# RWKV attention and GELU feed-forward on one core: the preparation in another order with common scales, the mix for V first in three steps, and three last steps with orders of their own

## The chip, the core and the metric

The program runs on one core of a Trainium2 chip. The metric is the device time of one launch in microseconds (us). A core has five engines that run side by side: TensorE (PE, matmuls and transposes; its weight loads are listed as PEld), VectorE (DVE), ScalarE (ACT), GpSimd (POOL) and SyncE (SP, which here only issues DMAs). They meet through semaphores: an instruction may wait for a count and may raise one when it is done.

## What is computed

x is 4 sequences of 2048 tokens with 512 channels, in float32. Two layers are added to it. The first is an RWKV attention with 32 heads of 16 channels, in chunks of Q = 64 tokens; the second is a feed-forward layer with 2048 hidden units.

```python
x = x + attention(layernorm(x))
x = x + ffn(layernorm(x))

def attention(x):                        # xx is the token before, minus x
    xk, xv, xr, xg = (x + xx * time_maa[m] for m in "kvrg")
    r, k, v = xr @ Wr.T, xk @ Wk.T, xv @ Wv.T      # split in 32 heads
    g = silu(xg @ Wg.T)
    w = exp(-exp(time_decay)); ws = w ** Q; wk = w ** (Q - 1 - i); wb = w ** i
    # per chunk of 64 tokens, carried on by the state:
    att = rc @ kc * w_mat                # w_mat: powers of w below the diagonal, time_faaaa on it
    yc = att @ vc + rc @ state * wb
    state = ws * state + kc * wk @ vc
    return (groupnorm(y) * gamma + beta) * g @ Wo.T

def ffn(x):
    D = gelu(float16(x) @ W0.T + bias0)
    return float16(float16(D) @ W1.T + bias1)
```

## The kernel before

**Tiling.** The 8192 tokens go in nb = 32 blocks of BT = 256 (NT = 2 tiles of 128). Products in float32 precision are made of three float16 passes over a high and a low part (`PASSES`); ACT writes the high part (`..._hi`), DVE or POOL the low one (`..._lo`).

**Preparation (`prepare`).** A block of its own runs ahead of the steps. It loads the five attention weights (`raw`; K_, R_, V_, G_, O_ in this order), transposes them on PE into three PSUM buffers `tp` of 128x1024 each (half a weight), and ACT and DVE write them scaled to `WT`. A scale is a power of two from the largest sum of squares: ACT squares and sums a weight (`act_square`), POOL takes the maximum over partitions (`pool_most`), DVE makes the scale in six small steps (`dve_scale`). ACT also makes the decay tables with Exp (`act_exps`: 16 pieces of 128x64 and three small ones), which DVE finishes in `dve_tables`. The first block's layer norm, transposes (`pe_X`, `act_xT`) and mixes for K and R are made here too. The steps begin when all engines are done with this block.

**Steps.** `steps` runs over n = 0 to nb + 2. Step n does the attention of block n, the tail (group norm, gate, Wo, residual) of block n - 1, the first 12 of 16 weight units of the feed-forward of block n - 2 (`pe_up` 0 to 7, `pe_down` 0 to 3), and its last four units (`pe_down` 4 to 7) in step n + 1. So steps 32, 33 and 34 have no attention: step 32 has a tail and feed-forward work, step 33 feed-forward work, step 34 only the last four downs. In steps 0 and 1 the feed-forward weights are transposed and scaled in sixteen pieces (`pe_prepare`, `act_prepare`, `dve_prepare`), stored to DRAM and read back from step 2 on.

**Order.** It is written out by hand for each engine: `pe_step`, `dve_step`, `act_step`, `pool_step`, `sp_step`. In `dve_step` the first loop interleaves the small steps of the next block's layer norm (`dve_ln`), the mixes for V and G (`dve_mix(n, 2, ...)`, `dve_mix(n, 3, ...)`), `dve_K_lo` and the group norm of the block before (`dve_normalize`); `mix_lo(n, 2)`, for which `pe_V` waits, comes behind the loop. The mix buffers alternate, so the mix for V takes the one that K had.

**DMA.** The SP queue issues in order and waits in order. Feed-forward weights come in units of 512 KB through a ring of 5 (`sp_weights`, each waits until the unit five before it is used up); `sp_fx` transposes the normalised input `xh` to `xT`, for which `pe_up` 0 waits; the output of block n - 3 is stored from `x1`, and x is loaded into the same buffer for the next tail.

**PSUM.** `F` has two banks, used by up j in turn (j % 2), by the downs for the two token tiles t, and emptied by `act_gelu` and `dve_e`.

## Time and profile before

| what | value |
| --- | --- |
| median of 3 runs | 2199.86 us (2199.13 to 2201.25) |
| the profiled execution, device time | 2201.86 us |
| its span, first to last instruction | 2200.0 us |
| PE busy | 2099.5 us (95%) |
| DVE busy | 1878.6 us (85%) |
| ACT busy | 1077.8 us (49%) |
| POOL busy | 382.4 us (17%) |
| chain that ended last | PE 89%, DVE 2%, issue 1% |
| DMA | 437.53 MB, mean 199 GB/s |

The profiled execution took 2.0 us more than the median, and 1.9 us of its time lie outside the span. In a row of the timeline stand the start, the duration, the engine, the line of the kernel, the operation with its tiles, and in brackets how long the engine was idle before and what it waited for. Rows of the same kind that follow each other are merged (x4).

### The profile page before, as it was taken

To read this page: it belongs to the slowest core of one execution; us is meant where nothing else is said; L and a number is where in the kernel's file an instruction comes from. 1 tells how busy PE (TensorE), PEld (TensorE's weight loads), DVE (VectorE), ACT (ScalarE), POOL (GpSimd) and SP (SyncE) were. 2 spreads that over 40 slices of the span, in tenths; PEclk is the share of its full clock that TensorE was granted. 3 is DMA by queue.
4 is the path that set the end of the run, shared out by engine and by line. 5 is a ranking of instruction groups with operands and counts; after the bars stand their busy time and mean duration, and the time that the engine had idled before them with its cause. 6 is when DMAs were issued, how large, how long until landed. Compare 5 with 4: busy or idle time off the path is not lost.

```text
span 2200.0 us, 59109 instructions
## 1 busy us (share of the span) xinstructions
PE 2099.5 (95%) x24288; PEld 1508.5 (69%) x24288; DVE 1878.6 (85%) x4352; ACT 1077.8 (49%) x1882; POOL 382.4 (17%) x336
## 2 busy tenths in 40 slices
PE   3767999999999999999999999999999999999998
PEld 3555777776677777667777766777776677777664
DVE  6788988888998888899888889988888998888861
ACT  6554455545445554444555444455544445554441
POOL 1111112111111211111121111112111211211110
PEclk8888999999999999999999999999999999999999
DMA  6544566676556666655666665566666556666666
GB/s 202 163 154 147 177 202 213 215 216 205 179 184 200 215 214 216 205 181 183 201 214 214 217 201 185 181 201 215 214 217 201 182 182 203 214 214 208 198 215 206
DMA packets 282651, 437.53 MB, mean 199 GB/s; under 512 B 123536, under 2 KB 160912, under 8 KB 282384
## 3 DMA queue, kind: packets, MB, share of 16 engines
q1 hardware_dynamic: 280752, 433.55, 62.6%
q8 instruction: 193, 3.16, 0.6%
q14 instruction: 74, 0.61, 0.1%
q10 hardware_dynamic: 1632, 0.21, 0.1%
HBM read 316.24 MB, written 25.17 MB: 155 GB/s over the span
## 4 chain that ended last, share of the span: by engine, by line
PE 89%; DVE 2%; issue 1%; DMA 0%; ACT 0%; POOL 0%; POOLq 0%; ACTq 0%; SPq 0%; DVEq 0%
PE F L825 21%; PE F L839 20%; PE B L656 11%; PE B L805 7%; PE YT L684 7%; PE sc L656 7%; PE YT L656 3%; PE sc L714 3%; PE YT L735 2%; PE YT L778 2%; PE YT L754 2%; PE sc L697 1%; PE YT L738 1%; PE B L258 1%; PE YT L258 1%
## 5 line engine op out<-in xcount | busy, mean ns | idle before, releaser
L825 PE MATMUL F<-xT,ring 128*128 128x256 f16 x4096 | 489.1, 273 | 5.3 <-DMA xT<-xh 5.3
L839 PE MATMUL F<-ring,hT 128*128 128x512 f16 x2048 | 481.6, 379 | 4.8 <-ACT hT L1279 1.2
L825 PEld LDWEIGHTS F<-xT,ring 128*128 128x128 f16 x4096 | 396.7, 98 | 67.0 <-issue 6.8
L839 PEld LDWEIGHTS F<-ring,hT 128*128 128x128 f16 x2048 | 193.2, 98 | 209.0 <-issue 9.3
L247 ACT ACTIVATE mix<-mixf 128x1024 f16<-128x1024 f32 x128 | 135.2, 1056 | 326.7 <-DVE mixf L219 212.9
L1279 ACT ACTIVATE hT<-F,b,f_rho 128x256 f16<-128x256 f32 x512 | 260.6, 563 | 41.8 <-PE F L825 41.8
L219 DVE SCALAR_TENSOR_TENSOR mixf<-dx,maa,xnT 128x256 f32<-128x256 f32 x512 | 271.2, 556 | 0.1
L656 PE MATMUL B<-mix,WT 128*128 128x256 f16 x2304 | 270.2, 274 | 0.0
L1395 POOL TENSOR_TENSOR Shl<-S,Shl 128x512 f16<-128x512 f32 x128 | 153.8, 1202 | 655.0 <-ACT Shl L1246 655.0
L656 PEld LDWEIGHTS B<-mix,WT 128*128 128x128 f16 x2304 | 224.2, 98 | 36.5 <-issue 0.2
L251 DVE TENSOR_TENSOR mix<-mixf,mix 128x1024 f16<-128x1024 f32 x128 | 196.3, 1534 | 0.0
L1246 ACT ACTIVATE Shl<-S 128x512 f16<-128x512 f32 x128 | 80.1, 626 | 236.1 <-DVE S L1041 131.8
L656 PE MATMUL sc<-mix,WT 128*128 128x256 f16 x1536 | 181.6, 276 | 10.8 <-PEq L434 10.8
L684 PE MATMUL YT<-WT,mix 128*128 128x512 f16 x768 | 180.4, 386 | 10.2 <-DVE mix L251 10.2
L1018 DVE TENSOR_TENSOR att<-att 128x512 f16<-128x512 f32 x256 | 178.4, 736 | 7.5 <-ACT att L1240 7.4
L1012 DVE TENSOR_TENSOR att<-sc,wmask 128x512 f32<-128x512 f32 x256 | 164.2, 683 | 20.7 <-PE sc L714 20.7
L656 PEld LDWEIGHTS sc<-mix,WT 128*128 128x128 f16 x1536 | 151.9, 99 | 43.1 <-issue 11.3
L1400 POOL TENSOR_TENSOR x<-e,x 128x512 f32<-128x512 f16 x64 | 73.0, 1161 | 603.8 <-DVE e L1092 603.8
L805 PE MATMUL B<-WT,yg 128*128 128x512 f16 x768 | 176.2, 379 | 0.1
L1240 ACT ACTIVATE att<-att 128x512 f16<-128x512 f32 x256 | 148.5, 630 | 36.7 <-DVE att L1012 35.7
L684 PEld LDWEIGHTS YT<-WT,mix 128*128 128x128 f16 x768 | 76.0, 99 | 96.6 <-DVE mix L251 10.7
L805 PEld LDWEIGHTS B<-WT,yg 128*128 128x128 f16 x768 | 75.0, 98 | 83.9 <-DVE x L984 0.3
(168 smaller groups left out, 2955.4 us busy)
## 6 DMA issues: line engine op xcount, KB each, us to landing
ring<-w_dram SPq DMA_DIRECT2D x512, 512.0 KB, 4.3
kx<-kT SPq DMA_DIRECT2D x96, 256.0 KB, 2.4
rx<-rT SPq DMA_DIRECT2D x96, 256.0 KB, 4.2
xa<-in_L_attn_x SPq DMA_DIRECT2D x32, 512.0 KB, 7.4
vbd<-vN SPq DMA_DIRECT2D x256, 64.0 KB, 3.7
x<-in_L_attn_x SPq DMA_DIRECT2D x32, 512.0 KB, 5.2
out<-x SPq DMA_DIRECT2D x32, 512.0 KB, 4.8
ring<-in_L_ffn_W SPq DMA_DIRECT2D x10, 512.0 KB, 8.8
```

Of the source, the lines that this page charges most:

```text
L219: last = eng.scalar_tensor_tensor(out=mixf[:, m % 2, g, :], in0=dx[:, g, :], scalar=maa[:, m, g:g + 1], in1=xnT[:, g, 1:BT + 1], op0=ALU.m ...
L251: eng.tensor_tensor(mix[:, m % 2, 1, :, :], mixf[:, m % 2, :, :], mix[:, m % 2, 0, :, :], ALU.subtract).then_inc(s_ml, 1)
L656: mm = eng.matmul(out[:, gg * BT:(gg + 1) * BT], WT[:, w, a, kk, rows(g)], mix[:, m % 2, b, kk, :], start=(i == 0 and kk == 0), stop=(i == ...
L684: mm = eng.matmul(Y[:, t, :], mix[:, 0, a, kk, rows(t)], WT[:, V_, b, kk, :], start=(i == 0 and kk == 0), stop=(i == 2 and kk == G - 1))
L805: mm = eng.matmul(B[:, :], yg[:, a, kk, rows(t)], WT[:, O_, b, kk, :], start=(i == 0 and kk == 0), stop=(i == 2 and kk == G - 1))
L825: mm = eng.matmul(F[:, j % 2, i * BT:(i + 1) * BT], ring[:, use % RING, i, a * C + kk * P:a * C + (kk + 1) * P], xT[:, :, kk, :], start=(k ...
L839: mm = eng.matmul(F[:, t, :], hT[:, k, rows(t)], ring[:, use % RING, i, a * C:(a + 1) * C], start=(k == 0 and a == 0), stop=(k == NH - 1 a ...
L1012: eng.tensor_tensor(att32[:, x, :], sc[:, x, :], wmask[:, 8 * x:8 * x + 8, :].rearrange("p q i -> p (q i)"), ALU.mult).then_inc(s_am, 1)
L1018: eng.tensor_tensor(att[:, c % 2, 1, C * x:C * x + C], att32[:, x, :], att[:, c % 2, 0, C * x:C * x + C], ALU.subtract).then_inc(s_al, 1)
L1240: eng.activation(att[:, c % 2, 0, C * x:C * x + C], att32[:, x, :], ACT.Copy).then_inc(s_ah, 1)
L1279: eng.activation(hT[:, k, :], F[:, j % 2, i * BT:(i + 1) * BT], ACT.Gelu, bias=b0[:, k:k + 1], scale=f_rho[:, j:j + 1]).then_inc(s_h, 1)
L1395: eng.tensor_tensor(Shl[:, b, 1, :], S[:, :], Shl[:, b, 0, :], ALU.subtract).then_inc(s_Sl, 1)
```

## The change

In the preparation the scales are made for two groups, K with R and V with G and O (`TOGETHER`), so POOL has 2 reductions in place of 5 and DVE 2 chains of six small steps in place of 5. A weight's ACT pass to `WT` waits for its group's chain. ACT's Exp pieces move from the end to the front, in two halves; the transposes of x stand behind those of K on PE; DVE makes the decay tables ahead of the second scale chain, and the factors from the scales (`dve_factors`) behind it.

ACT, preparation, before (`junk,sums<-raw` is a square, `WT<-tp` and `WT<-YT` a half weight, `xa` the normalised block, `wmask` the Exp pieces):

```order
L227 ACTIVATE xa<-xa,ln_n,ln_r 128x512 x2
L238 ACTIVATE xnT<-B 128x4x128
L238 ACTIVATE xnT<-YT 128x4x128
L350 ACTIVATE junk,sums<-raw 128x2048 x2
L247 ACTIVATE mix<-mixf 128x1024
L369 ACTIVATE WT<-tp,scl 128x1024 x2
L247 ACTIVATE mix<-mixf 128x1024
L350 ACTIVATE junk,sums<-raw 128x2048
L369 ACTIVATE WT<-YT,scl 128x1024
L369 ACTIVATE WT<-tp,scl 128x1024
```

and now:

```order
L389 ACTIVATE wmask<-tabs,ep 128x64 x8
L352 ACTIVATE junk,sums<-raw 128x2048
L228 ACTIVATE xa<-xa,ln_n,ln_r 128x512 x2
L352 ACTIVATE junk,sums<-raw 128x2048
L239 ACTIVATE xnT<-B 128x4x128
L239 ACTIVATE xnT<-YT 128x4x128
L389 ACTIVATE wmask<-tabs,ep 128x64 x8
L393 ACTIVATE wb<-wb 128x32
L394 ACTIVATE wk<-wk 128x32
L395 ACTIVATE ws<-ec 128x4
L375 ACTIVATE WT<-tp,scl 128x1024 x2
```

The square of K stands ahead of the norm, that of R ahead of the copies of x's transposes, and the Exp pieces that came ahead of the last weight stand in two halves at the front.

DVE, the end of the preparation and the start of step 0, before (`L431` is the last factor, `L219` a mix for V):

```order
L431 TENSOR_SCALAR out_scale<-out_scale 128x1
L434 UNCONDITIONAL_BRANCH
L1556 UNCONDITIONAL_BRANCH
L189 BN_STATS bn<-xa 128x6
L219 SCALAR_TENSOR_TENSOR mixf<-dx,maa,xnT 128x256
L189 BN_STATS bn<-xa 128x6
L219 SCALAR_TENSOR_TENSOR mixf<-dx,maa,xnT 128x256
L193 BN_AGGR mv<-bn 128x2
```

and now (`L383` is the low part of half a weight, `L435` to `L447` the factors, `L220` a mix, `L252` a low part of a mix, `L1003` K's low part):

```order
L447 TENSOR_SCALAR out_scale<-out_scale 128x1
L383 SCALAR_TENSOR_TENSOR WT<-tp,scl,WT 128x1024
L383 SCALAR_TENSOR_TENSOR WT<-YT,scl,WT 128x1024
L383 SCALAR_TENSOR_TENSOR WT<-tp,scl,WT 128x1024 x2
L383 SCALAR_TENSOR_TENSOR WT<-YT,scl,WT 128x1024
L383 SCALAR_TENSOR_TENSOR WT<-tp,scl,WT 128x1024
L450 UNCONDITIONAL_BRANCH
L1647 UNCONDITIONAL_BRANCH
L220 SCALAR_TENSOR_TENSOR mixf<-dx,maa,xnT 128x256 x4
L190 BN_STATS bn<-xa 128x6 x2
L194 BN_AGGR mv<-bn 128x2 x2
L1003 SCALAR_TENSOR_TENSOR kT<-sc,kT 128x512
```

The factors stand ahead of the last six low parts of weights instead of behind them, and the four mixes for V stand together at the front of the step. Behind K's low part follow one small step and the low part of the mix for V, which stood behind the whole loop before. The same holds in steps 1 and 2.

PE, from the end of step 31 to the end, before (`L839` are downs, 8 matmuls each; `L825` ups, 16 each; `L697` the transposes of y; `L805` a half of Wo):

```order
L839 MATMUL F<-ring,hT 128x512 x40
L825 MATMUL F<-xT,ring 128x256 x32
L697 MATMUL sc<-ident,y 128x128 x8
L825 MATMUL F<-xT,ring 128x256 x96
L805 MATMUL B<-WT,yg 128x512 x12
L839 MATMUL F<-ring,hT 128x512 x16
L805 MATMUL B<-WT,yg 128x512 x12
L839 MATMUL F<-ring,hT 128x512 x48
L825 MATMUL F<-xT,ring 128x256 x128
L839 MATMUL F<-ring,hT 128x512 x64
```

and now:

```order
L880 MATMUL F<-ring,hT 128x512 x40
L723 MATMUL sc<-ident,y 128x128 x8
L851 MATMUL F<-xT,ring 128x256 x96
L831 MATMUL B<-WT,yg 128x512 x12
L851 MATMUL F<-xT,ring 128x256 x16
L831 MATMUL B<-WT,yg 128x512 x12
L851 MATMUL F<-xT,ring 128x256 x16
L880 MATMUL F<-ring,hT 128x512 x64
L851 MATMUL F<-xT,ring 128x256 x128
L880 MATMUL F<-ring,hT 128x512 x32
L867 MATMUL F<-ring,hT 128x512 x32
```

The transposes of y stand ahead of all ups, both halves of Wo ahead of the downs, and the last 32 matmuls go tile by tile. On the SP queue the transpose of `xh` stands in steps 32 and 33 ahead of the weight units instead of behind three of them, and the last store is two of 256 KB. On DVE, step 32 has the group norm ahead of `dve_e`; the last residual sum is made by DVE (a tile at a time) instead of POOL. In every step the first down waits for the last two GELU pieces only at its second tile.

The diff, cut:

```diff
+TOGETHER = ((K_, R_), (V_, G_, O_))
...
-        def pool_most(eng, u):
-            eng.wait_ge(s_sum, ORDER.index(u) + 1)
...
+        def pool_most(eng, k):
+            at = columns(TOGETHER[k])
+            eng.wait_ge(s_sum, ORDER.index(TOGETHER[k][-1]) + 1)
+            eng.partition_all_reduce(sums[:, at], sums[:, at], P, bass.bass_isa.ReduceOp.max).then_inc(s_all, 1)
...
+        def dve_ep(eng):
+            eng.wait_ge(s_e0, 1)
...
             @block.tensor
-                for t in range(NT):
-                    pe_X(eng, 0, t)
...
+                    if u == K_:
+                        for t in range(NT):
+                            pe_X(eng, 0, t)
...
             @block.vector
                 for k in range(LN_STEPS):
                     dve_ln(eng, 0, k)
+                    if k == NT - 1:
+                        dve_ep(eng)
                 eng.memset(xnT[:, :, 0:1], 0.0).then_inc(s_carry, 1)
                 dve_exponents(eng)
+                dve_scale(eng, 0)
                 eng.wait_ge(s_maa, 64)
                 dve_dx(eng, 0)
-                for m in range(2):
-                    for g in range(G):
-                        dve_mix(eng, 0, m, g)
-                for u in ORDER:
-                    dve_scale(eng, u)
+                for g in range(G):
+                    dve_mix(eng, 0, 0, g)
+                dve_lo(eng, K_)
+                for g in range(G):
+                    dve_mix(eng, 0, 1, g)
+                mix_lo(eng, 0, 0)
+                dve_lo(eng, R_)
+                dve_tables(eng)
+                dve_scale(eng, 1)
+                mix_lo(eng, 0, 1)
+                dve_factors(eng)
+                for u in (V_, G_, O_):
                     dve_lo(eng, u)
...
     def pe_down(eng, f, j):
-        if j == 0:
-            eng.wait_ge(s_h, NH * (f + 1))
...
+                if k == 0:
+                    eng.wait_ge(s_h, NH * (f + 1) - 2 * (NT - 1 - t))
...
+    def pe_after_attention(eng, n):
+        for j in range(4, 8):
+            pe_down(eng, n - 3, j)
+        pe_yT(eng, n)
+        for j in range(6):
+            pe_up(eng, n, j)
+        pe_Wo(eng, n, 0)
+        pe_up(eng, n, 6)
+        pe_Wo(eng, n, 1)
+        pe_up(eng, n, 7)
+        for j in range(4):
+            pe_down(eng, n - 2, j)
...
     def dve_step(eng, n):
-        if not att_n:
+        if n > nb:
             dve_e(eng, n - 3)
+        early = n <= 2
         for k in range(LN_STEPS):
+            if early and k == 0:
+                for g in range(G):
+                    dve_mix(eng, n, 2, g)
             if ahead:
                 dve_ln(eng, n + 1, k)
-            if att_n:
+            if early:
+                if k in (3, 9):
+                    dve_K_lo(eng, n, (3, 9).index(k))
+                elif k == 4:
+                    mix_lo(eng, n, 2)
+                elif 5 <= k < 9:
+                    dve_mix(eng, n, 3, k - 5)
+            elif att_n:
...
     def sp_step(eng, n):
+        if n >= nb and ff:
+            sp_fx(eng, n - 2)
         if late:
             sp_weights(eng, use)
             sp_weights(eng, use + 1)
             sp_weights(eng, use + 2)
-        if ff:
+        if n < nb and ff:
             sp_fx(eng, n - 2)
```

## Rows read from the trace of the kernel before

**Rows 1.** Windows of us: busy us and (xcount) of each engine, PEclk, DMA share, GB/s:
```profile
222.00:252.00 30.00, 29.84 (x455) 21.18 (x455) 28.97 (x50) 15.67 (x28) 5.89 (x5) 1.00 0.56 191
```

**Rows 2.** Timeline of ACT in the preparation: start us, us, engine, line, operation:
```profile
11.26 1.52 ACT L227 ACTIVATE xa<-xa,ln_n,ln_r 128x512 f32<-128x512 f32 x2 [3.13 <-DVE ln_n L204]
...
13.41 0.60 ACT L238 ACTIVATE xnT<-B 128x512 f32<-128x512 f32 x1 [0.63 <-PE B L258]
...
16.78 1.91 ACT L350 ACTIVATE junk<-raw 128x2048 f32<-128x2048 f32 x1
...
18.69 1.04 ACT L247 ACTIVATE mix<-mixf 128x1024 f16<-128x1024 f32 x1
...
20.45 2.12 ACT L369 ACTIVATE WT<-tp,scl 128x1024 f16<-128x1024 f32 x2 [0.72 <-DVE scl L301]
...
38.94 3.92 ACT L383 ACTIVATE wmask<-tabs,ep 128x64 f32<-128x64 f32 x16
```

**Rows 3.** R's four loads (ns, first and last issue), and the last one's landing:
```profile
L342 SPq DMA_DIRECT2D raw<-in_L_attn_Wr x4: 603/604/1688, 9.0 to 12.1; - x4
...
raw<-in_L_attn_Wr SPq DMA_DIRECT2D x1, 256.0 KB, 3.9
```

**Rows 4.** Timeline of DVE at the end of the preparation:
```profile
45.50 1.28 DVE L377 SCALAR_TENSOR_TENSOR WT<-tp,scl,WT 128x1024 f16<-128x1024 f32 x1
...
49.57 0.15 DVE L419 TENSOR_TENSOR gn_eps<-rho 128x1 f32<-128x1 f32 x1
...
50.65 0.15 DVE L431 TENSOR_SCALAR out_scale<-out_scale 128x1 f32<-128x1 f32 x1
```

**Rows 5.** Timeline of PE: K's 48 matmuls in step 0 and in step 2:
```profile
51.49 8.29 PE L656 MATMUL sc<-mix,WT 128*128 128x256 f16 x48 [10.84 <-PEq L434]
...
187.01 5.41 PE L656 MATMUL sc<-mix,WT 128*128 128x256 f16 x48
```

**Rows 6.** Timeline of PE: V's first tile in step 1 and in step 2:
```profile
134.00 2.76 PE L684 MATMUL YT<-WT,mix 128*128 128x512 f16 x12 [2.13 <-DVE mix L251]
...
205.70 5.30 PE L684 MATMUL YT<-WT,mix 128*128 128x512 f16 x12 [8.03 <-DVE mix L251]
```

**Rows 7.** Timeline of DVE in step 2:
```profile
194.11 0.68 DVE L189 BATCH_NORM_STATS2 bn<-xa 128x6 f32<-128x512 f32 x1
...
211.04 0.69 DVE L995 TENSOR_TENSOR vw<-YT,wk 128x512 f32<-128x512 f32 x1 [4.20 <-PE YT L684]
...
222.02 1.23 DVE L210 TENSOR_TENSOR dx<-xnT 128x1024 f32<-128x1024 f32 x1 [0.59 <-ACT xnT L238]
```

**Rows 8.** The chain that ended last, ahead of a first down in step 29:
```profile
1975.53 0.12 issue
```

**Rows 9.** Timeline of all engines, steps 32 to 34:
```profile
2120.35 1.27 SPq L1460 DMA_TRANSPOSE xT<-xh  x1
...
2123.51 0.67 DVE L955 TENSOR_REDUCE gn_s<-yi 128x32 f32<-128x512 f32 x1
...
2124.46 3.65 PE L825 MATMUL F<-xT,ring 128*128 128x256 f16 x32 [2.31 <-DMA xT<-xh]
...
2129.01 1.17 PE L697 MATMUL sc<-ident,y 128*128 128x128 f32 x8 [0.90 <-DVE y L973]
...
2162.68 15.80 PE L825 MATMUL F<-xT,ring 128*128 128x256 f16 x128 [3.02 <-DMA xT<-xh]
...
2179.68 13.97 PE L839 MATMUL F<-ring,hT 128*128 128x512 f16 x64 [1.20 <-ACT hT L1279]
2193.69 1.41 DVE L1092 SCALAR_TENSOR_TENSOR e<-F,f_rho,b 128x512 f16<-128x512 f32 x2 [32.58 <-PE F L839]
2194.52 2.27 POOL L1400 TENSOR_TENSOR x<-e,x 128x512 f32<-128x512 f16 x2 [31.72 <-DVE e L1092]
2196.82 0.39 SPq L1501 DMA_DIRECT2D out<-x  x1
```

**Rows 10.** DMAs issued in 185.9 to 186.3 us, KB each, us to landing:
```profile
ring<-w_dram SPq DMA_DIRECT2D x1, 512.0 KB, 4.8
```

## What the change will do to the time, as predicted

> **What bounds the kernel now.** I read the windows first. In 222 to 252 us PE is busy 29.84 of 30 us and DVE 28.97 [rows 1]; the page gives PE 95% and the chain that ended last 89% on PE. From step 3 to step 31 PE has no gap to give back, and the change leaves that order as it is. What can be had lies in three places where PE waits: the preparation, in which K's first matmul starts only at 51.49 [rows 5]; steps 1 and 2, where V waits for the mix [rows 6]; and steps 32 to 34, where PE waits for transposes, GELU and y, and where 6.3 us follow PE's last matmul [rows 9]. So I read the timelines of ACT and DVE in the preparation, of DVE and PE at V, and of all engines behind 2115.
>
> **The preparation.** Before, every weight runs a loop of its own: square, reduction, six small DVE steps, high part, low part; then come tables and factors, and K waits for all of it. Now ACT works in a row, and I follow it. R's last load is issued at 12.1 and lands 3.9 later, at 16.0 [rows 3]. What ACT has ahead of R's square (8 Exp pieces, K's square, the norm of 1.5) fits before that: ep is ready near 8.9, and 1.9 + 2.1 + 1.5 bring it to about 14.5, if K is there by 11 or so. From 16.0 ACT has, by its rows [rows 2]: R's square 2.1 (1.91 and the read of the sum), two copies of x's transposes 1.2, the other 8 Exp pieces 1.9 and three small ones 0.4, K's high part 2.0, a mix 1.0, V's square 2.1, R's high part 2.0, the squares of G and O 4.2. That is 16.9, so 32.9. From the end of R's square (18.78) to the first high part (20.45) passed 1.67: the reduction and the small steps. So V, G and O have scales at 34.5. DVE then has the low part of the mix for R (1.15) and the factors, 49.57 to 50.80, 1.25 [rows 4], and is at 36.9. Six low parts of weights follow, 1.2 apart (45.50 to 46.69) and 1.28 for the last: 44.2. The high parts and transposes fit in between. K started 0.7 behind DVE's last step (50.80 to 51.49), so now at about 44.8: **6.7 us less**. The six low parts are DVE's alone, so this is the sum of two chains that don't overlap. Bounds: R's square was done at 16.78 without a wait for it to be seen, so at latest it starts there, 0.8 later (5.9 less); had the loads of R landed a little earlier than their last one, 1.2 more (7.9). The decay tables (46.78 to 49.57, 2.8) are hidden: DVE has nothing else between R's low part, near 30.3, and the second reduction. If that cover went, they would cost up to 2.8.
>
> ACT goes Exp, square, identity, Exp now. After one table load at the start the profile shows none at the second run of Exp at 38.94, which stands behind squares and identities [rows 2].
>
> The Trainium skill ("ScalarE: Activation LUTs", on table sets) says to group functions by their table set, and prices each switch at about 2.7 us; by that rule splitting Exp in two could cost some switches. The row speaks for one set here.
>
> K's 48 matmuls took 8.29 in step 0, behind 10.84 us of an idle PE, and 5.41 in step 2 [rows 5]: the granted clock was at its lower level, 1.2 GHz, at first. Now PE idles about 3 us ahead of K, but does little in the 10 us before that too. I take K as it was, and keep 0 to 3 us for the range.
>
> **Step 0.** V's mix comes first, but V waits for PE there, not the mix. DVE now holds at the mix's low part until ACT can write the high part, which needs both halves of K. Behind DVE at that wait are the mixes for G, K's second low part and the layer norm; who waits for them is ACT, whose norm comes behind eight squares, and the SP queue, whose K stacks go out some 3 us later. Both have that much slack by my walk through the step. Cost 0 (0 to 1).
>
> **Steps 1 and 2.** In step 1 V starts 2.13 late [rows 6]. With the mix's low part inside the loop V follows R at once, but DVE needs as long as before for the same loop, plus about 0.4 for ACT. DVE then waited for V and now doesn't: **1.0 us less** (0 to 2.1). In step 2 V waited 8.03 and then ran at half speed, 5.30 for what took 2.76 in step 1 [rows 6]. DVE reaches the loop at 194.1 [rows 7]. Four mixes, two statistics, a variance, four small steps, K's low part and the mix's low part make 6.5, so V starts at 200.6 instead of 205.7, 3 us behind R, I take it at full speed. But DVE ends its loop at 206.8 as before, and then lay idle 4.20 until V was done [rows 7]. That idle time is what is gained at first. Through V's high and low parts, the second product, the gate and ACT's queue (GELU of unit 1, four pieces of the gate, the copies of x) I come to dx at 218.1 instead of 222.02, and as PE is then no longer what DVE waits for, 0.7 more: **4.6 us less**. From there to the next K DVE is busy 28.97 of 30 [rows 1], so PE gets no more than DVE does. Bounds: 2.9, if ACT's queue holds the gate back, and 7.7, V's whole delay and slow clock.
>
> **Steps 3 to 31.** Only the split wait at the first down is new, once a step. The GELU it waits for is long done, as Wo and other work lie between. There is a gap of 0.12 ahead of that down today [rows 8]. Taking it away would give 3.5 in 29 steps, doubling it cost 3.5; I take 0, since the number of waits ahead of the first matmul is the same.
>
> **Steps 32 to 34.** (a) y. The group norm runs from 2123.51 to the transposes at 2129.01 [rows 9], 5.5; it now starts at 2118.9, right behind y's square, and y is there at about 2123.4. The e of the block before comes behind it, near 2124.1, and frees the bank for the first up at 2124.8. Before, ups started at 2124.46 and PE lay idle 2.31 and 0.90. (b) The weights. Now the transpose of xh goes first and has to wait for ACT until 2120.35 [rows 9]; the units 0 to 2, issued before from 2115.3 on, stand behind it. The first is issued at 2121.65. Five units in a row showed 4.8 to landing for the first [rows 10]; with 4.8 that is 2126.4, and I take 2126.2, so the wait only changes its name: ups start at 2126.2 with y's transposes done. Then PE has 6 ups of 1.75 (two took 3.65, the end of the last matmul among it [rows 9]), Wo 2.6, an up, Wo, an up, 8 downs of 1.73 (eight took 13.97): 33.05, to 2159.3. Before, that point was 2159.65. **0.4 less** (0.5 more to 1.7 less). Waiting behind the weights on SP: store of the last block, x's load for the residual, near 2138.5, needed at 2139.3. (c) Wo is now done 5.5 us earlier, so xh of the last block is transposed by 2156.6 in place of 2162.6. The next up waits for e alone, 0.85, and starts at 2160.1 in place of 2162.68: **2.2 less**. (d) Those eight ups took 15.80 with 3.02 idle ahead of them [rows 9]; with 0.85 idle I take 8 x 1.75 = 14.0: **1.8 less**. (e) The first two matmuls of the down go ahead of the last GELU, of a wait of 1.20: **0.6 less** with the trace's rounding. (f) The end. From PE's last matmul, 2193.65, it was 1.41 for e, POOL's second sum to 2196.79, the store to 2200.0: 6.35. Now e of one tile 0.75, DVE's sum 0.7, store 3.2 less what half the bytes save: 4.75, **1.6 less**. If POOL's 1.16 were what DVE takes too, 1.1; if the store halves, 2.8. The ring's last unit is issued when the third last-step down is done and is needed some 4.3 later, a stall of 0.1 to 0.5 that I leave out. Sum **6.6** (4.4 to 8.5).
>
> For the halved store the Trainium skill ("DMA: Bandwidth & Descriptors", on the anatomy of one DMA) gives about 2.0 us fixed and 436 GB/s, so half of 512 KB would save an estimated 0.6 of its 3.2; the trace here has no store of 256 KB to out.
>
> **The sum.** 6.7 + 0 + 1.0 + 4.6 + 0 + 6.6 = 18.9 us. Against the profiled execution that is 2201.86 - 18.9 = 2183.0 (span 2181.1); it lay 2.0 above the median, so the median becomes 2199.86 - 18.9 = **2181.0**.
>
> **The rivals.**
> - K and the rest of step 0 run at the upper clock, as PE now idles 3 us and not 11: up to 3 less, 2178. For it: V at full speed behind 2.13 idle. Against it: PE's thin work ahead.
> - Step 2 gives little: ACT's queue, not DVE, brings dx to where it was, and only the 0.7 is left: 2185.
> - The weights of step 32 land one after the other later than PE uses them, and x's load behind them holds the second Wo. (a) to (c) then give about nothing, the rest stays: 3 more, 2184. With the rival before, 2188.
> - A table switch at each change between Exp and the rest, by a load such as the one in the preparation of 1.28 (four of them) on ACT's chain: 5 more, 2186. The row at 38.94 speaks against it. The Trainium skill's rule on table sets, cited above, speaks for it.
> - Slower: the new wait between the two tiles of the first down makes PE's queue stop in each of 30 steps. At 0.7 each it is 21 us, 2202; it decides from 0.63 on. The gap there is 0.12 now, and nothing of that size is seen.
>
> **Chances.** Forecast (2178.5 to 2184.5) 0.53; upper clock 0.12; step 2 gives little 0.12; weights late 0.08, both together 0.04; table switches 0.01; slower 0.02; larger misses on either side 0.08. The range is 2174 to 2188.5: the forecast, both bounds of preparation and last steps, and the rivals up to 2188; below 2174 two upper bounds would have to meet. A run can tell about 0.2% (4.4 us) from no change. Faster by more 0.96, within 0.02, slower 0.02.
>
> **What would show it.** K's first matmul near 44.8; V in step 2 near 193 (200.6 less the 6.7 and 1.0 before), with no idle DVE before its product; the distance from K of step 3 to the end of step 31 unchanged within 1 us; in step 32 one wait of PE for the ring, not for xT; no low clock in step 33; 4.8 from PE's last matmul to the end. A first matmul later than 47, or a step of more than 64.3 us, would make the forecast wrong.

## The result, and the profile after

| | before | after |
| --- | --- | --- |
| median, device time | 2200.35 us (2199.13 to 2201.25, 4 runs) | 2184.99 us (2184.25 to 2185.52, 4 runs) |
| profiled execution, its span | 2201.86, 2200.0 us | 2184.56, 2182.7 us |
| K's first matmul in step 0 | 51.49 | 45.94 |
| step 0, step 1, step 2 (from K to K) | 68.72, 66.80, 68.12 | 67.11, 67.75, 62.70 |
| K of step 3 to the 40 downs at the end of step 31 | 1858.21 | 1857.96 |
| from those 40 downs to the end of the span | 86.66 | 81.24 |

The ratio is 0.993 with a 95% interval of 0.9913 to 0.9948: 15.4 us faster, and the spans differ by 17.3. A step is counted from the first matmul of its K to that of the next. The prediction of 2181.0 is 4.0 too low and its range of 2174 to 2188.5 holds the result.

The page of the changed kernel, busy time by engine and the chain that ended last:

```profile
PE 2098.8 (96%) x24288; PEld 1509.8 (69%) x24288; DVE 1874.7 (86%) x4336; ACT 1077.7 (49%) x1882; POOL 378.7 (17%) x331
...
PE 59%; DVE 28%; issue 4%; ACT 2%; DMA 0%; DVEq 0%; ACTq 0%
```

PE and DVE do the same work as before, in a span that is 17 us shorter. That the chain runs 28% over DVE now and ran 89% over PE before goes with no change of time: steps 3 to 31 took 1858.21 before and 1857.96 now. In such steps both engines are busy nearly all the time [rows 1], and my reading, which no run tests, is that the chain goes down the one or the other by a small margin.

**Preparation.** Timeline of the changed kernel, from the last groups of transposes (`L489`) to K (`L682`); `L375` is a high part on ACT, `L383` a low part on DVE. Columns as ahead of the prediction:

```profile
37.62 1.97 PE L489 MATMUL tp<-ident,raw 128*128 128x128 f32 x8 [6.04 <-DVE WT L383]
...
39.38 1.92 PE L489 MATMUL YT<-ident,raw 128*128 128x128 f32 x8
39.62 1.11 ACT L375 ACTIVATE WT<-tp,scl 128x1024 f16<-128x1024 f32 x1 [2.65 <-PE tp L489]
...
41.09 1.91 PE L489 MATMUL tp<-ident,raw 128*128 128x128 f32 x8
...
44.18 1.28 DVE L383 SCALAR_TENSOR_TENSOR WT<-tp,scl,WT 128x1024 f16<-128x1024 f32 x1
...
45.94 7.07 PE L682 MATMUL sc<-mix,WT 128*128 128x256 f16 x48 [2.94 <-PEq L450]
```

K comes 5.55 earlier than [rows 5] had it, not 6.7. The factors and the decay tables no longer stand at the end of DVE's work [rows 4]. But ACT, and DVE behind it, wait for transposes. Each group of eight takes 1.9, and PE was idle for 6.04 ahead of them.

**Step 1.** Timeline of the changed kernel: DVE's low part of the mix for V (`L252`), V's first tile (`L710`), GpSimd's reduction (`L613`), DVE's first step that reads its result (`L292`), GpSimd's first `vw` (`L1498`), and DVE's second product (`L1056`), which writes what GpSimd reads:

```profile
120.78 1.23 DVE L252 TENSOR_TENSOR mix<-mixf,mix 128x1024 f16<-128x1024 f32 x1 [0.84 <-ACT mix L248]
...
124.67 2.75 PE L710 MATMUL YT<-WT,mix 128*128 128x512 f16 x12
...
129.20 0.38 POOL L613 PARTITION_ALL_REDUCE f_most<-f_most  x1 [14.11 <-DVE f_most L617]
...
131.06 0.14 DVE L292 TENSOR_SCALAR f_rho<-f_most 128x1 f32<-128x1 f32 x1
...
137.13 1.14 POOL L1498 TENSOR_TENSOR vw<-vw 128x512 f16<-128x512 f32 x1 [7.55 <-issue]
...
138.37 0.69 DVE L1056 TENSOR_TENSOR vw<-YT,wk 128x512 f32<-128x512 f32 x1 [2.55 <-POOL vw L1498]
```

V starts at once, but DVE then waits 2.55 for GpSimd, and GpSimd, for 7.55, for nothing that the profile shows. DVE reads the result of the reduction at 131.06, so the 7.55 are not the reduction itself. The same two rows in the kernel before:

```profile
143.42 1.26 POOL L1413 TENSOR_TENSOR vw<-vw 128x512 f16<-128x512 f32 x1 [7.57 <-issue]
```

```profile
144.78 0.69 DVE L995 TENSOR_TENSOR vw<-YT,wk 128x512 f32<-128x512 f32 x1 [1.12 <-POOL vw L1413]
```

**Step 2.** Timeline of the changed kernel, V on PE and DVE's work behind it, to be laid beside [rows 6, 7]:

```profile
193.77 4.45 PE L710 MATMUL YT<-WT,mix 128*128 128x512 f16 x12 [2.31 <-DVE mix L252]
...
200.62 0.68 DVE L1056 TENSOR_TENSOR vw<-YT,wk 128x512 f32<-128x512 f32 x1
...
211.29 1.23 DVE L211 TENSOR_TENSOR dx<-xnT 128x1024 f32<-128x1024 f32 x1 [0.60 <-ACT xnT L239]
```

V waits 2.31 in place of 8.03, DVE's 4.20 of idle time is gone, and dx stands 10.7 earlier.

**Steps 32 to 34.** Timeline of PE in the changed kernel, from the 40 downs on (`L880`; `L851` ups, `L867` the last downs, tile by tile), to be laid beside [rows 9]:

```profile
2101.46 8.81 PE L880 MATMUL F<-ring,hT 128*128 128x512 f16 x40
2111.71 1.17 PE L723 MATMUL sc<-ident,y 128*128 128x128 f32 x8 [1.45 <-DVE y L1034]
2114.06 5.41 PE L851 MATMUL F<-xT,ring 128*128 128x256 f16 x48 [1.18 <-DMA ring<-w_dram]
2119.98 5.40 PE L851 MATMUL F<-xT,ring 128*128 128x256 f16 x48 [0.51 <-ACT hT L1360]
...
2133.89 0.59 PE L880 MATMUL F<-ring,hT 128*128 128x512 f16 x2
2135.17 13.56 PE L880 MATMUL F<-ring,hT 128*128 128x512 f16 x62 [0.68 <-ACT hT L1360]
2149.66 14.13 PE L851 MATMUL F<-xT,ring 128*128 128x256 f16 x128 [0.94 <-DVE e L1156]
...
2164.91 6.65 PE L880 MATMUL F<-ring,hT 128*128 128x512 f16 x30 [0.68 <-ACT hT L1360]
2171.39 7.36 PE L867 MATMUL F<-ring,hT 128*128 128x512 f16 x32
```

And the last store, issue by issue: before one of 512 KB, after two of 256 KB (KB each, us to landing):

```profile
out<-x SPq DMA_DIRECT2D x1, 512.0 KB, 2.8
```

```profile
out<-x SPq DMA_DIRECT2D x2, 256.0 KB, 2.0
```

The waits for xT are gone, and small ones have come: for a weight, for GELU at the fourth up and at both first downs. PE's last matmul ends at 2178.75, and the span 3.95 later, where it was 6.35.

### The profile page after: what moved, and what is told of

It is laid out like the page before. It is cut to its first block, busy times and chain, and to the rows that moved or that the text cites. A ratio compares the mean times of both kernels' runs of the same rounds, so it can differ in the third digit from the quotient of the medians.

```text
span 2182.7 us, 59086 instructions
## 1 busy us (share of the span) xinstructions
PE 2098.8 (96%) x24288; PEld 1509.8 (69%) x24288; DVE 1874.7 (86%) x4336; ACT 1077.7 (49%) x1882; POOL 378.7 (17%) x331
## 4 chain that ended last, share of the span: by engine, by line
PE 59%; DVE 28%; issue 4%; ACT 2%; DMA 0%; DVEq 0%; ACTq 0%
PE F L880 13%; PE F L851 13%; PE B L682 7%; PE sc L682 7%; PE YT L710 7%; DVE mixf L220 6%; DVE att L1079 5%; DVE mix L252 4%; PE YT L682 3%; DVE S L1102 3%; DVE att L1073 3%; DVE kv L1088 2%; PE sc L740 1%; PE sc L723 1%; PE YT L804 1%
## 5 line engine op out<-in xcount | busy, mean ns | idle before, releaser
L851 PE MATMUL F<-xT,ring 128*128 128x256 f16 x4096 | 487.6, 273 | 2.6 <-DMA ring<-w_dram 1.2
L880 PE MATMUL F<-ring,hT 128*128 128x512 f16 x2016 | 475.2, 379 | 1.4 <-ACT hT L1360 1.4
L851 PEld LDWEIGHTS F<-xT,ring 128*128 128x128 f16 x4096 | 395.5, 98 | 63.7 <-issue 2.2
L880 PEld LDWEIGHTS F<-ring,hT 128*128 128x128 f16 x2016 | 189.7, 98 | 200.5 <-ACT hT L1360 2.3
L220 DVE SCALAR_TENSOR_TENSOR mixf<-dx,maa,xnT 128x256 f32<-128x256 f32 x512 | 270.4, 555 | 0.4 <-PEq L450 0.3
L682 PE MATMUL B<-mix,WT 128*128 128x256 f16 x2304 | 269.7, 274 | 0.0
L682 PEld LDWEIGHTS B<-mix,WT 128*128 128x128 f16 x2304 | 224.1, 98 | 36.0
L252 DVE TENSOR_TENSOR mix<-mixf,mix 128x1024 f16<-128x1024 f32 x128 | 196.2, 1533 | 3.1 <-ACT mix L248 3.0
L682 PE MATMUL sc<-mix,WT 128*128 128x256 f16 x1536 | 180.5, 275 | 2.9 <-PEq L450 2.9
L710 PE MATMUL YT<-WT,mix 128*128 128x512 f16 x768 | 179.6, 384 | 2.3 <-DVE mix L252 2.3
L682 PEld LDWEIGHTS sc<-mix,WT 128*128 128x128 f16 x1536 | 151.5, 99 | 34.6 <-issue 3.5
L1321 ACT ACTIVATE att<-att 128x512 f16<-128x512 f32 x256 | 148.5, 630 | 36.9 <-DVE att L1073 35.8
L710 PEld LDWEIGHTS YT<-WT,mix 128*128 128x128 f16 x768 | 75.9, 99 | 88.2 <-issue 4.6
```

Source lines behind the costliest of these rows:

```text
L220: last = eng.scalar_tensor_tensor(out=mixf[:, m % 2, g, :], in0=dx[:, g, :], scalar=maa[:, m, g:g + 1], in1=xnT[:, g, 1:BT + 1], op0=ALU.m ...
L252: eng.tensor_tensor(mix[:, m % 2, 1, :, :], mixf[:, m % 2, :, :], mix[:, m % 2, 0, :, :], ALU.subtract).then_inc(s_ml, 1)
L682: mm = eng.matmul(out[:, gg * BT:(gg + 1) * BT], WT[:, w, a, kk, rows(g)], mix[:, m % 2, b, kk, :], start=(i == 0 and kk == 0), stop=(i == ...
L710: mm = eng.matmul(Y[:, t, :], mix[:, 0, a, kk, rows(t)], WT[:, V_, b, kk, :], start=(i == 0 and kk == 0), stop=(i == 2 and kk == G - 1))
L851: mm = eng.matmul(F[:, j % 2, i * BT:(i + 1) * BT], ring[:, use % RING, i, a * C + kk * P:a * C + (kk + 1) * P], xT[:, :, kk, :], start=(k ...
L880: mm = eng.matmul(F[:, t, :], hT[:, k, rows(t)], ring[:, use % RING, i, a * C:(a + 1) * C], start=(k == 0 and a == 0), stop=(k == NH - 1 a ...
```

## The experiments

The sum of the prediction has five stretches, so every kernel is read in the same five. The table gives them from one profile each, in us.

| kernel | K starts | step 0 | step 1 | step 2 | 3 to 31 | last steps | span |
| --- | --- | --- | --- | --- | --- | --- | --- |
| before | 51.49 | 68.72 | 66.80 | 68.12 | 1858.21 | 86.66 | 2200.0 |
| after | 45.94 | 67.11 | 67.75 | 62.70 | 1857.96 | 81.24 | 2182.7 |
| e_prep | 46.75 | 67.59 | 67.91 | 68.21 | 1858.12 | 87.32 | 2195.9 |
| e_front | 51.44 | 68.35 | 68.32 | 62.05 | 1858.08 | 84.56 | 2192.8 |
| e_tail | 51.42 | 68.18 | 67.00 | 67.75 | 1858.13 | 82.42 | 2194.9 |
| e_pool | 46.65 | 67.55 | 64.58 | 62.69 | 1858.17 | 80.86 | 2180.5 |
| e_only2 | 46.04 | 66.90 | 69.05 | 62.07 | 1857.97 | 82.37 | 2184.4 |
| e_warm | 45.82 | 67.11 | 67.13 | 62.70 | 1857.97 | 81.47 | 2182.2 |
| e_unit | 45.98 | 67.11 | 69.37 | 62.07 | 1857.97 | 79.90 | 2182.4 |
| e_tail2 | 46.78 | 67.11 | 67.03 | 62.70 | 1857.95 | 79.13 | 2180.7 |
| e_sum | 46.63 | 67.11 | 66.51 | 62.06 | 1858.00 | 78.39 | 2178.7 |
| e_best | 45.15 | 65.44 | 65.22 | 62.70 | 1858.09 | 78.70 | 2175.3 |

Kernels with the same code in a stretch show how far a profile can be trusted there. From step 3 to step 31 they differ by less than 0.3. In steps 1 and 2 together the five with the order of the changed kernel (after, e_front, e_warm, e_unit, e_tail2) lie between 129.7 and 131.4. A difference of less than 1.7 us there is told only where a row shows it. With the new preparation K starts between 45.8 and 46.8, and at 45.15 in e_best. Most of this spread is R's load: R's square, which waits for it, began between 15.59 and 16.56. Counted from GpSimd's second reduction K starts 14.0 to 14.2 later in seven profiles, 13.55 in e_warm and 12.75 in e_best, the two with idle transposes.

### One part alone

`e_prep` is the kernel before with the new preparation, `e_front` with the mix for V first in steps 0 to 2, `e_tail` with the new last steps and the split wait. So the diff of each is the part of the change's diff that stands ahead of the prediction.

> The kernel before with the new preparation alone (common scales, Exp pieces first, the factors ahead of the last six low parts); steps and last steps as before. Theory 'separate': the gain of the preparation adds to the rest. K's first matmul at 45.9, step 0 shorter by 1.2 to 1.6 since K's 48 matmuls take 7.1 in place of 8.3, then nothing: span 2200.0 - 5.55 - 1.4 = 2193.0, steps 1 and 2 as before (66.8 and 68.3 from K to K). Theory 'clock lost later': the 1.6 of step 0 came with V's mix first; then step 0 stays 68.7 and the span is 2194.4.

> The kernel before with the mix for V first in steps 0 to 2 alone. Theory 'separate': K's first matmul 51.5 and 8.3 long; step 0 within 0.5 of 68.7; step 1 longer by 0.9 (67.7), since GpSimd, not V, holds the second product of vw in both kernels; step 2 5.6 shorter (62.7). Span 2200.0 - 4.8 = 2195.2. Theory 'step 1 lost by the preparation' (some piece stands differently behind it): step 1 is 65.8 as predicted and the span 2193.3.

> The kernel before with the new last three steps and the split wait at the first down alone. Theory 'separate': from the first down of step 31's units (2113.3 in the kernel before) to the end 5.4 less than the 86.7 of before, and nothing ahead of it: span 2194.6. Theory 'split wait costs or gives': the stretch from step 3 to step 31 differs by 1 us or more from before.

Measured against 2201.15 us: e_prep 2195.67 (ratio 0.9976, 0.9967 to 0.9985), e_front 2194.58 (0.9972, 0.9961 to 0.9982), e_tail 2197.31 (0.9986, 0.9976 to 0.9995). That is 5.5, 6.6 and 3.8, together 15.9 where the whole change gave 15.4: the parts add, as far as times that are known to about 2 us each can tell. The spans were 2195.9, 2192.8 and 2194.9, where 2193.0, 2195.2 and 2194.6 were expected. So 'separate' missed twice in size: e_prep by 2.9 (K 0.85 later than expected, and the rest in steps 0 and 1 and the last steps), e_front by 2.4, of which 2.1 lie in its last steps. By the table:

- Step 0 is shorter with the new preparation (67.59) and not with V's mix first (68.35; e_tail, which changes nothing there, has 68.18). Its gain comes with the preparation.
- Step 1 is no shorter in any of them. With V's mix first it is 68.32, as 'separate' had it but for 0.6.
- Step 2 owes its gain to V's mix first alone: 62.05.
- The split wait at the first down shows nothing in 29 steps: 1858.13 against 1858.21.

In e_front the last steps, with the code of before, took 84.56, in the kernel before 86.66, in e_prep 87.32. The cause stands in the 128 ups of step 33, PE's timeline, in e_front and in e_prep:

```profile
2157.12 14.13 PE L825 MATMUL F<-xT,ring 128*128 128x256 f16 x128 [2.56 <-DMA xT<-xh]
```

```profile
2158.56 15.80 PE L851 MATMUL F<-xT,ring 128*128 128x256 f16 x128 [2.74 <-DMA xT<-xh]
```

It is the clock for 1.67 of the 2.1. In the kernel before, these ups took 15.80 too [rows 9], and in the windows of 4 us its granted clock (third from the right) is 0.64 at first, so for the most part the lower level of 1.2 GHz, and then 1.00:

```profile
2164.00:2168.00 4.00, 4.00 (x26) 3.06 (x24) 0.00 (x0) 1.02 (x2) 0.00 (x0) 0.64 0.82 292
2168.00:2172.00 4.00, 4.00 (x39) 3.59 (x38) 0.00 (x0) 2.52 (x6) 0.00 (x0) 1.00 0.71 206
```

The slow start came behind an idle PE of 2.56 to 3.02 in two of three profiles, and behind the 0.94 of the new order in none of nine. So the 1.67 are a cost that the old order has often, not always, and the profile of before, from which the prediction took its terms, is one that had it.

### V's mix first in step 2 only

```diff
-        early = n <= 2
+        early = n == 2
```

> The changed kernel with the mix for V first in step 2 alone; steps 0 and 1 have the loop of before. Theory 'the order in step 1 holds the reduction back': with the old order VectorE reaches the largest sum at 15.2 behind K's first matmul and not at 15.9, so GpSimd's first vw ends near 24.0 and not at 25.2, and the second product starts at 24.6 to 25.0 in place of 25.3; V in turn starts late again. Step 1 then takes 66.8 to 67.9 (as in the kernel before and in the one with the new preparation alone), so the order in step 1 was worth nothing or a small loss. Step 0 is within 0.5 of 67.1 (its order is worth nothing, its gain is the clock at K). Step 2 is 62.7 as before it. Rival 'the order in step 1 gains the 1.0 of the prediction and something else lost it': step 1 gets longer than 68.7.

2185.31 us, 0.9929 (0.9915 to 0.9944): as the changed kernel, 2184.99. GpSimd's reduction comes at 15.14 behind K and not at 16.15, so the first half of the theory holds. The second product waits for nothing, but it comes at 25.06, beyond the 24.6 to 25.0 expected and within the 24.6 to 25.4 of the five kernels with the other order: what the order takes from the reduction, the varying time behind it hides. Step 1 took 69.05, which is beyond the 68.7 set for the rival. But e_unit, with V's mix first and the code of the changed kernel there, took 69.37, so this profile decides nothing against the order. What can be said is that steps 1 and 2 took 131.12 together, within the 129.7 to 131.4 of the kernels with the mix first in all three: in steps 0 and 1 the edit is worth nothing that a profile shows, and its whole gain is in step 2.

### GpSimd's reduction earlier

```diff
+            if n == 1:
+                act_piece_square(eng, 1, 7)
             act_mix_hi(eng, n, 3)
-            if n == 1:
-                act_piece_square(eng, 1, 7)
...
                 elif 5 <= k < 9:
                     dve_mix(eng, n, 3, k - 5)
+                if n == 1 and k == 8:
+                    dve_piece_most(eng)
...
-            if n == 1:
-                dve_piece_most(eng)
```

> The changed kernel with one thing more in step 1: ScalarE squares piece 7 of the second weight ahead of the mix for G (it is idle for 2.0 there), and VectorE takes the largest sum right behind the last mix for G, not behind the low parts of R. So GpSimd's reduction over the partitions can start near 124.9 in place of 129.2. Theory 'GpSimd is slow from a reduction to the next elementwise operation' (7.6 passed between them, without a wait): its first vw of step 1 ends near 134 in place of 138.3, VectorE's second product starts without the wait of 2.55, and step 1 is shorter by 1.5 to 2.5 (67.75 to about 65.7), span about 2180.7. Rival 'the pieces of the weight set the end of step 1': the wait goes, but V1's piece and those behind it are no earlier, and step 1 stays within 0.5 of 67.75. Second rival 'the 7.6 are a wait for ScalarE's high part': GpSimd's vw stays near 137.1.

Timeline of e_pool in step 1, GpSimd and DVE's second product:

```profile
124.82 0.38 POOL L613 PARTITION_ALL_REDUCE f_most<-f_most  x1 [8.59 <-DVE f_most L617]
132.14 1.15 POOL L1498 TENSOR_TENSOR vw<-vw 128x512 f16<-128x512 f32 x1 [6.94 <-issue]
...
135.94 0.68 DVE L1056 TENSOR_TENSOR vw<-YT,wk 128x512 f32<-128x512 f32 x1
```

The first `vw` came 5.0 earlier (6.1 counted from K), 6.94 behind the reduction, while ACT's high part was ready at the same time as before (130.45 + 0.62, in the changed kernel 130.24 + 0.62). So it isn't ACT that GpSimd waits for. DVE's wait of 2.55 is gone and step 1 took 64.58. Steps 1 and 2 together are 127.27 here, 128.57 and 127.92 in the two kernels below with the same edit, and 129.7 to 131.4 without it. That is a gain of about 2.5, on the mean of the three against that of the five. A part of it may be the clock: the piece that PE transposes behind DVE's work took 1.94 behind an idle 6.04 in the changed kernel, and 1.06 behind 3.41 in e_pool; but in e_sum, below, it took 1.94 behind 3.40. The device time, 2184.60 (0.9929, 0.9913 to 0.9946), doesn't show the gain. Nor does the span of 2180.5: the profiled execution, 2182.29, was the fastest of four, and the others took up to 2185.79. The evidence is the wait that is gone, and the two steps in three profiles.

### TensorE kept busy in the preparation

```diff
+                        if at == 7:
+                            eng.wait_ge(s_xT, NT)
+                            for i in range(40):
+                                eng.transpose(B[:, rows(i % G)], ident[:, :], ident[:, :])
                         if at >= 3:
                             eng.wait_ge(s_lo, at - 2)
```

> The changed kernel with 40 idle transposes of the unit matrix on TensorE (into a PSUM bank that is free there) between the transposes of 30.5 us and those of 37.6, where TensorE is idle for 6.0. They change nothing that is computed. Theory 'the last three groups of transposes were slow by the clock': they take 1.04 to 1.2 each in place of 1.9, ScalarE's waits for them (2.65, 0.96, 0.23) shrink by about 1.3 in all, the last low part ends near 44.2 in place of 45.46 and K starts near 44.7 (45.94 before), span 1.2 less or a little more, as K's first matmuls may keep the upper clock too. Rival 'VectorE's and ScalarE's turns set the end': the transposes get shorter, but K starts within 0.3 of 45.9.

Timeline of PE in e_warm: the idle transposes (`L483`), then the last three groups (`L493`):

```profile
32.05 4.53 PE L483 MATMUL B<-ident 128*128 128x128 f32 x40
38.16 1.09 PE L493 MATMUL tp<-ident,raw 128*128 128x128 f32 x8 [1.57 <-DVE WT L383]
39.44 1.73 PE L493 MATMUL YT<-ident,raw 128*128 128x128 f32 x8 [0.19 <-DVE WT L383]
40.96 1.91 PE L493 MATMUL tp<-ident,raw 128*128 128x128 f32 x8
```

Half a hit. The first group runs at the upper clock, the second only in part, the third not at all. From the start of the first group to K it took 7.66, and 8.32 in the changed kernel: 0.7 gained where 1.2 was expected. K itself, at 45.82, is only 0.12 earlier, since R's square began 0.55 later in this profile. The device time, 2183.49 (0.9923, 0.9908 to 0.9938), can't tell so little.

### The first weight ahead of the transpose of xh

```diff
+        if n == nb:
+            sp_weights(eng, use)
         if n >= nb and ff:
             sp_fx(eng, n - 2)
         if late:
-            sp_weights(eng, use)
+            if n != nb:
+                sp_weights(eng, use)
```

> The changed kernel with the first weight unit of step 32 issued ahead of the transpose of xh, which waits for ScalarE; units 1 and 2 behind it as now. Theory 'TensorE waits 1.18 for a weight that stands behind the transpose': the first up starts right behind y's transposes, 1.1 to 1.2 earlier (11.4 behind the first down of step 31's last units, 12.6 now), units 1 and 2 arrive in time, and the stretch from that down to the end is 80.1 in place of 81.2, if nothing behind takes it back. Rival 'the wait changes its name again': xT or the bank that e frees is no earlier than 12.5, and the first up starts within 0.2 of now. Second rival: unit 1, issued at 8.3 as now, makes a wait between the first two ups of over 0.5.

Timeline of PE in e_unit, y's transposes and the first ups of step 32:

```profile
2112.75 1.17 PE L723 MATMUL sc<-ident,y 128*128 128x128 f32 x8 [1.45 <-DVE y L1034]
2114.01 5.40 PE L851 MATMUL F<-xT,ring 128*128 128x256 f16 x48
```

The ups start without a wait, 11.51 behind the start of the 40 downs (2102.50) in place of 12.60. The changed kernel's profile was a late one there: the other five with its SP order have 12.05 to 12.22, so the edit is worth 0.5 to 1.1. Nothing takes it back: the last steps are 79.90, 1.3 less, 0.3 of it because the last weight was there in time. Median 2184.17, ratio 0.9924 (0.9908 to 0.9941).

### Three small waits of the last steps

```diff
+        if n == nb:
+            act_gated(eng, n - 1)
         if ff:
             act_gelu(eng, n, 0)
...
-        if n == nb:
-            act_gated(eng, n - 1)
...
+        places = [(i, t) for i in range(2) for t in range(NT)]
+        if j == 0 and f >= nb - 2:
+            places = [(i, t) for t in range(NT) for i in range(2)]
...
         f = nb - 1
+        pe_down(eng, f, 4)
         for t in range(NT):
-            for j in range(4, 8):
+            for j in range(5, 8):
```

> The changed kernel with three small things in the last steps, each at one wait that the prediction had missed or left out. In step 32 ScalarE applies y's scale ahead of the first GELU (it idles 7.6 there) and not behind it: the wait of 0.51 ahead of the fourth up goes. In steps 32 and 33 the first down does two units of work for the first tile before it starts on the second: the waits of 0.68 for the last GELU go to 0.25. In step 34 the first unit is done for both tiles and only the last three tile by tile, so that the last unit is needed 0.9 later: the wait of about 0.45 for it goes. Theory 'these three waits are the miss of the last steps': the stretch from step 31's last downs to the end is 1.8 shorter, 79.4 in place of 81.2. Rival 'they sit on something else': each wait comes back at the next instruction, and the stretch stays within 0.5 of 81.2.

Timeline of PE in e_tail2, steps 32 to 34:

```profile
2113.79 10.65 PE L851 MATMUL F<-xT,ring 128*128 128x256 f16 x96 [0.80 <-DMA ring<-w_dram]
...
2134.23 13.12 PE L883 MATMUL F<-ring,hT 128*128 128x512 f16 x60 [0.25 <-ACT hT L1363]
...
2163.54 7.94 PE L883 MATMUL F<-ring,hT 128*128 128x512 f16 x36 [0.25 <-ACT hT L1363]
2171.32 5.34 PE L868 MATMUL F<-ring,hT 128*128 128x512 f16 x24
```

Each of the waits is gone or down to 0.25, and the last weight is there when it is needed. The last steps took 79.13, 2.1 less than the 81.24; 0.4 of it is an earlier landing of the first weight (12.22 behind the downs), so about 1.7 are the edit's. Median 2183.25, ratio 0.992 (0.9905 to 0.9935).

### Together

`e_sum` has the edits of e_pool, e_unit and e_tail2. `e_best` has more idle transposes besides, 50 in the gap and 12 behind the last group.

> The changed kernel with the earlier reduction in step 1, the first weight unit of step 32 ahead of the transpose of xh, and the three small things of the last steps, together. Theory 'they add': K's first matmul at 46.0 to 46.8, steps 1 and 2 together 127.3 (129.7 to 131.4 in the four profiles without the reduction moved), step 3 to step 31 unchanged (1858.1), and from step 31's last downs to the end 81.2 - 1.1 - 1.7 = 78.4: span 2177.0 to 2178.5, 4.7 less than the changed kernel's 2182.7, device time near 2180. Rival 'the earlier reduction was a lucky clock': steps 1 and 2 take 129.7 or more and the span is over 2180.

> The same as the one before it, with idle transposes of the unit matrix on TensorE in the preparation: 50 in the gap ahead of the last three groups of transposes (40 of them left 1.57 idle, and only the first group ran at the upper clock), and 12 behind the last group, so that K starts with less idle time ahead. Theory 'the clock holds if TensorE is busy up to the groups': all three groups take about 1.1, the last low part ends 1.2 earlier, K's first matmul is near 44.9 to 45.5, its 48 matmuls take less than 6.0 in place of 7.1, and the span is 2 less than without: 2175 to 2176.5. Rival 'the clock isn't to be had so cheaply': the groups or K stay slow, K starts within 0.4 of the run beside it. Second rival: the 50 end too late and delay the first group; then K is later.

Timeline of PE in e_best, from the idle transposes (`L483`, `L499`) to K:

```profile
32.23 5.62 PE L483 MATMUL B<-ident 128*128 128x128 f32 x50
38.28 1.09 PE L493 MATMUL tp<-ident,raw 128*128 128x128 f32 x8 [0.43 <-DVE WT L383]
39.56 1.06 PE L493 MATMUL YT<-ident,raw 128*128 128x128 f32 x8 [0.19 <-DVE WT L383]
40.67 1.09 PE L493 MATMUL tp<-ident,raw 128*128 128x128 f32 x8
41.59 1.47 PE L499 MATMUL B<-ident 128*128 128x128 f32 x12
45.15 5.40 PE L688 MATMUL sc<-mix,WT 128*128 128x256 f16 x48 [2.08 <-PEq L450]
```

Stretches of 8 us, PEclk is the third number from the right: the changed kernel, and e_best:

```profile
36.00:44.00 8.00, 5.38 (x24) 4.99 (x24) 6.32 (x7) 4.17 (x4) 0.00 (x0) 0.57 0.39 75
44.00:52.00 8.00, 6.06 (x41) 4.84 (x42) 5.71 (x12) 5.23 (x10) 6.23 (x5) 0.79 0.01 2
```

```profile
36.00:44.00 8.00, 6.41 (x53) 5.49 (x51) 7.48 (x13) 4.88 (x5) 0.00 (x0) 1.00 0.33 60
44.00:52.00 8.00, 6.85 (x63) 6.19 (x64) 6.11 (x12) 6.33 (x11) 6.23 (x5) 1.00 0.01 2
```

e_sum took 2180.15 us (0.9908, 0.9892 to 0.9925), e_best 2177.90 (0.9899, 0.9884 to 0.9914), against 2200.39. The edits add: 78.39 for the last steps (78.4 expected), and a span of 2178.7. In e_best, with PE busy up to the groups the clock stays at 2.4 GHz, all three groups take 1.1, K starts 1.5 earlier than in e_sum (whose reductions came at the same time within 0.04), and its 48 matmuls take 5.40. Step 0 is shorter by just those 1.67 (65.44 against 67.11). e_best is 7 us faster than the changed kernel by their medians (2177.90 and 2184.99, each beside its own runs of the kernel before, which agree to 0.1), and the best of all.

## Why the prediction was right, and where it was off

The spans differ by 17.3 where the sum says 18.9, so the terms are 1.6 too good. Larger misses cancel in that: the 1.6 of step 0, which the sum had at nothing, and 0.8 of step 2 make up for more than half of the 4.3 that were missed the other way: 1.95 in step 1 and 1.2 each in the preparation and the last steps. The other 2.4 of the miss of 4.0 is no term: the profiled execution of before lay 2.0 above the median that was known, that of the changed kernel 0.4 below its own. The median of 2184.99 lies 0.5 outside the forecast of 2178.5 to 2184.5 and on the 2185 that stood for the rival 'step 2 gives little'. That is chance: step 2 gave more than its term.

| step | predicted | measured | |
| --- | --- | --- | --- |
| preparation | -6.7 (-7.9 to -5.9) | -5.55 (-4.7 to -5.5 in six other profiles of it) | low clock of the transposes |
| step 0 | 0 | -1.6 | K's clock, the rival |
| step 1 | -1.0 (-2.1 to 0) | +0.95, within the spread of 0 | GpSimd |
| step 2 | -4.6 (-7.7 to -2.9) | -5.4 | hit |
| steps 3 to 31 | 0 (3.5 either way) | -0.25 | hit |
| steps 32 to 34 | -6.6 (-8.5 to -4.4) | -5.4 | see below |

**Preparation: the mechanism was right, a term was mis-sized.** R's square was seen at 15.59 and its end at 17.6; the second scale chain ended at 33.8 (34.5 predicted), the factors at 36.2 (36.9), the last two 0.7 ahead of the working. The 0.7 is R's load (0.4) and ACT's row of work, 16.0 in place of 16.9, less 0.5 for a wrong reading: from the last square's end to the scales it took 2.2, not 1.67. Before, the first high part at 20.45 had not waited for R's square. It waited for K's scale, whose small steps DVE began only at 19.33, behind eight mixes. What failed is the sentence that the high parts and transposes fit in between six low parts 1.2 apart. They had been read from before, where PE's gaps ahead of these groups were 2.4 to 3.0 and the groups took 1.1. With all squares ahead of them the gap is 6.04 and a group takes 1.9, so the six low parts took 9.2 and not 7.3. e_warm and e_best show that most of it was the clock: in e_best, with PE busy, the groups take 1.1, the six low parts 7.7, and K starts 1.45 earlier, counted from the reduction. The rest, 0.4, is mostly a wait of 0.35 for ACT that e_best still has.

The rule that the prediction weighed here, the Trainium skill's ("ScalarE: Activation LUTs", on table sets), cost nothing: the trace of the changed kernel has one table load in the preparation, at 4.63, and none between Exp, squares, identities and the second half of Exp. The same section of the Trainium skill has copy and identity in every set, which speaks against the rival too and was not weighed; the square it doesn't name there. The row of before was the better witness.

**Step 0: the rival came, in part.** K took 7.07 and not 8.29, which is 1.2 of the 1.6. It had been given 0.12 with up to 3. With no low clock at all, in e_best, K takes 5.40 and the step is 3.3 shorter than before: the rival's bound was right, and fewer idle us ahead of K were not enough by themselves, since behind 2.94 K still started slowly.

**Step 1: the step that failed.** V started at once, as predicted. The term took it that DVE's wait for V was the only one on the way. The rows of before that speak against it, shown above beside step 1, were in reach: there the second product already waited 1.12 for GpSimd's `vw`, which came 7.57 behind the reduction. V's mix first makes DVE wait 0.84 for ACT's high part, and the reduction comes 16.15 behind K where it was 15.3 (15.6 to 16.2 in the five profiles, 15.1 to 15.3 in the four with the old order). What DVE gains at the first product (0.7) it waits at the second. Whether the order costs anything in step 1, the spread hides. e_pool took the reduction out of the way and gained about 2.5.

The Trainium skill ("GPSIMD Engine Reference", 2.1 Instruction dispatch) says that the first call of freshly loaded GpSimd code pays about 6 us with no instruction in the profile. The 6.8 to 8.1 between a reduction and the next elementwise operation in steps 0 and 1 of all profiles here fit it in kind, a little above in size. That it is code being loaded, no row shows.

**Step 2: right.** V's first matmul came at 193.77, for 193; no idle DVE ahead of V's product; dx 10.7 earlier, 4.5 of it by this step (3.9 predicted), and 0.9 more behind it (0.7). V ran slow (4.45), against the "full speed" that was taken, and it cost nothing, since DVE was not there before V's end. The rival that ACT's queue holds the gate back didn't come.

**Steps 3 to 31: right.** Within 0.3 in ten more profiles. The slower rival, a stop of PE in each split wait, is shown false by e_tail, which has the wait: its 29 steps took 1858.13.

**Steps 32 to 34, by the letters of the prediction.** (a) held: y's transposes stand ahead of the ups. (b) was to give 0.4 and cost 1.0: the downs of step 32 ended 47.27 behind the 40 downs, and 46.31 before. The ups started at 12.60 (12.86 predicted, for just the reason given), but there is a wait of 0.51 for GELU behind ACT's scale of y, and one of 0.68 at the first down, because the last up now stands right before it. Before, Wo and its neighbours stood between. This is a cover lost by a move. The prediction says that Wo and other work lie between for steps 3 to 31, and has no such wait in the sum of step 32. PE's own work there was 33.5, not 33.05. (c) gave 2.1, for 2.2. (d) gave 1.7, for 1.8, but as e_front shows it is a clock that the old order gets in some executions only. (e) gave 0.5, for 0.6. The last weight's stall, left out as 0.1 to 0.5, took 0.3. (f) gave 2.4, for 1.6: e of one tile saved 0.65 and DVE's sum 0.95, as in the working, and the store 0.8. For the store the sum had nothing: its own terms, 0.75, 0.7 and 3.2, make 4.65 without any saving, and it wrote 4.75. The Trainium skill's estimate for the halved store, 0.6 ("DMA: Bandwidth & Descriptors", on the anatomy of one DMA), stood beside the sum; the section gives it for DMAs that GpSimd issues, and this one is SP's. It would have brought this term nearer, though not the whole sum: the measured landing went from 2.8 to 2.0.

## What to carry to other kernels

Where a wait is taken away, follow the engine that now comes early to its next wait in the old trace: the wait of 1.12 for GpSimd was in the rows, and it was all that step 1 had to give. Where work is packed closer on two engines, look at what it does to the third one's gaps: here TensorE stood still for 6.04 in place of 2.4 to 3.0, and three short groups of transposes then took 1.9 each in place of 1.1. And in a tail that is put in a new order, each move takes a cover from somebody: go over the pairs that have become neighbours.

## What the runs showed of the hardware

- A GpSimd elementwise operation behind a partition reduction started 6.8 to 8.1 us after its end in step 1 of all twelve profiles, whatever else was ready. The reduction itself is listed with 0.4, and in the changed kernel VectorE read its result 1.5 us behind it.
- The last gap alone doesn't tell at which clock TensorE starts. Behind an idle 2.94 to 2.96 K's 48 matmuls took 7.07 in five profiles; behind 2.08, with idle transposes ahead, 5.40. Behind 1.57 a group of eight transposes still ran at 1.09, and the one right behind it at 1.73. In step 1 a group of eight behind 3.40 to 3.41 took 1.06 in e_pool and e_best and 1.94 in e_sum. In step 32 the same first ups, behind gaps of 1.45 and about 0.7, took 5.41 in most profiles and 7.03 and 7.08 in e_only2 and e_tail.
- The last store, of 256 KB, landed 2.0 us after its issue in nine profiles, one of 512 KB 2.8 us after in three.
